# Attention's first fetches on two issuing engines, batch 1 fetched behind the first maxima's rows, and TensorE's branch moved ahead of its waits

## The reference

```python
x = x + L0_xattn(layernorm(x), ctx, ctx, mask, Wq, bq, Wk, bk, Wv, bv, Wo, bo)   # key mask
x = x + L0_ffn(layernorm(x), ternary_weight, bias, act_scale)
x = x + L1_xattn(layernorm(x), ctx, ctx, W_q, W_k, W_v, b_v, W_o, b_o)           # strictly causal, row 0 sees key 0
x = x + L1_ffn(layernorm(x), w_gate, w_up, w_down)                               # gated, fake-quantized
```

## Time and profile before

| | us |
|---|---|
| median of 3 runs | 1466.51 |
| lowest and highest | 1465.78, 1467.19 |
| the profiled execution | 1467.55 |
| its span, first to last instruction | 1465.8 |
| mean granted TensorE clock in it | 0.946 of full speed |

### The profile page before, as it was taken

How to read it: one execution, slowest core, us unless ns; L and a number is a source line. 1 busy time by engine, 2 the same in 40 slices (tenths; PEclk the granted TensorE clock), 3 DMA queues, 4 the chain that set the end, 5 groups by cost and what they waited for, 6 DMA issues and landing times. The chain is left out here.

```text
span 1465.8 us, 21139 instructions
## 1 busy us (share of the span) xinstructions
PE 1307.9 (89%) x7327; PEld 643.9 (44%) x7327; DVE 951.1 (65%) x1647; ACT 849.5 (58%) x1489; POOL 424.0 (29%) x639
## 2 busy tenths in 40 slices
PE   8999945999999999999999989999995999970498
PEld 4655521333434434344455445544543444430387
DVE  5444415888787887877666687877762343996532
ACT  3544420777676776777755655555553446869432
POOL 0000000013543444345465433333331001648300
PEclk9999975999999999999999999999996999985699
DMA  8768656132342434423424553333210001316132
GB/s 293 248 252 289 239 166 188 45 96 60 94 122 75 121 84 121 123 80 88 111 83 120 154 153 88 96 112 96 57 39 17 0 0 43 133 82 258 43 101 86
DMA packets 87916, 170.75 MB, mean 116 GB/s; under 512 B 14586, under 2 KB 49157, under 8 KB 86277
## 3 DMA queue, kind: packets, MB, share of 16 engines
q1 hardware_dynamic: 87812, 169.42, 37.1%
HBM read 108.27 MB, written 60.31 MB: 115 GB/s over the span
## 5 line engine op out<-in xcount | busy, mean ns | idle before, releaser
L1202 DVE TENSOR_REDUCE b_neg_max<-b_score 128x1 f32<-128x512 f32 (+3 forms) x864 | 540.6, 663 | 218.6 <-PE b_score L765 108.5
L987 ACT ACTIVATE b_probs<-b_exp 128x512 f32<-128x512 f32 (+1 forms) x864 | 463.1, 582 | 307.5 <-PE b_exp L790 306.6
L765 PE MATMUL b_score<-b_k_stack,b_q_stack 97*128 97x512 bf16 (+3 forms) x1024 | 356.7, 352 | 34.1 <-issue 21.0
L790 PE MATMUL b_exp<-b_q_stack,b_k_stack 100*128 100x512 bf16 (+3 forms) x1024 | 345.0, 342 | 20.7 <-DMA b_q_stack<-b_max_rows 15.1
L811 PE MATMUL b_av<-b_probs,b_values 128*17 128x512 f32 (+3 forms) x2048 | 229.9, 521 | 3.6 <-POOL b_probs L1080 3.3
L765 PEld LDWEIGHTS b_score<-b_k_stack,b_q_stack 97*128 97x128 bf16 x1024 | 100.0, 98 | 271.0 <-DVE b_neg_max L1202 140.4
L1088 POOL CAST b_max_parts<-b_neg_max 128x16 bf16<-128x16 f32 x64 | 12.7, 198 | 506.6 <-DVE b_neg_max L1202 506.3
L790 PEld LDWEIGHTS b_exp<-b_q_stack,b_k_stack 100*128 100x128 bf16 x1024 | 100.4, 99 | 97.7 <-ACT b_probs L987 23.7
L1080 POOL TENSOR_SCALAR_AFFINE_SELECT b_probs<-b_probs 128x512 f32<-128x512 f32 x96 | 61.7, 643 | 184.6 <-ACT b_probs L987 184.3
L768 PE MATMUL b_score<-diag_qk,minus_big 128*128 128x128 bf16 x512 | 113.0, 221 | 0.0
L1746 PE MATMUL f_down<-f_w_downT,f_tmp 128*128 128x256 f32 x384 | 84.7, 384 | 4.6 <-DVE f_tmp L1423 4.6
(11 more groups left out here) (211 smaller groups left out, 1760.2 us busy)
## 6 DMA issues: line engine op xcount, KB each, us to landing
b_q_stack<-s_q SPq DMA_DIRECT2D x384, 64.0 KB
s_k<-a_part_k SPq DMA_DIRECT2D x48, 256.0 KB, 5.6
b_k_stack<-s_k SPq DMA_DIRECT2D x64, 192.0 KB
s_up<-f_up SPq DMA_DIRECT2D x6, 1536.0 KB, 5.1
s_va<-a_va SPq DMA_DIRECT2D x16, 544.0 KB, 5.0
b_values<-s_va SPq DMA_DIRECT2D x16, 544.0 KB, 4.3
a_mask_q<-mask_in SPq DMA_DIRECT2D x8, 1024.0 KB, 7.6
b_k_stack<-s_k SPq DMA_DIRECT2D x64, 128.0 KB
```

The source lines that it names most:

```text
L765: mm = pe.matmul(o, q, KS[half][0:R_MAX, h, 0:w], start=True, stop=causal or not general)
L790: mm = pe.matmul(o, k, QS[half][0:NSTACK, h, q0:T], start=True, stop=not masked)
L987: nc.scalar.activation(probs[kc][:, h0:h0 + m, q0:T], exp_bank[n % RINGS][:, 0:m * w].rearrange("p (h n) -> p h n", h=m), ACT.Exp).then_in ...
L1202: nc.vector.tensor_reduce(neg_max[u][:, qt, h0:h0 + m], score_bank[n % RINGS][:, 0:m * w].rearrange("p (h n) -> p h n", h=m), AX.X, ALU.ma ...
```

## The change

It has four parts.

1. A helper `keep_busy` issues matmuls of 128x128 weights against 128x512 constants whose result nobody reads. TensorE runs 20 of them at the end of the projections, and 20 at the start of attention's first slots, behind the branch.
2. TensorE reads the flag and branches first. The wait on `preset` stands behind the branch and the 20 matmuls; the wait on the rows of ones moves into the maxima, for groups 0 and 4 alone, and `rows_set` becomes one semaphore for each half of the stacks.
3. The first fetches are divided: SyncE issues the queries of batch 0's four groups, with values and masks behind group 1, and x; ScalarE issues keys and rows of ones, those of the second half last.
4. Batch 1's stacks are fetched by SyncE in slots -1 (groups 0, 1) and 0 (groups 2, 3, values, masks), in each behind the sending of the maxima's rows.

```diff
+def keep_busy(pe, const, psum, count):
+    for _ in range(count):
+        pe.matmul(psum[:, :], const["ident_b"][:, :], const["less"][:, :], start=True, stop=True)
@@ project_phase, tensor
             less(NB - 1, "q0", 2)
+            keep_busy(pe, const, out(NB - 1, 7), 20)
@@ attention_phase
-        ROWS_SET = 16 * 4
+        ROWS_SET = 16 * 2
+        def fetch_queries(eng, n, g):
+            h0, h1 = 4 * g, 4 * g + 4
+            for row, i in ((0, 0), (1, 0), (2, 0), (3, 1), (4, 1), (5, 2)):
+                eng.dma_start(QS[n % 2][HD * row:HD * (row + 1), h0:h1, :], scratch["q"][n][i][:, h0:h1, :]).then_inc(stack_landed[n % 2][g], 16)
+        def fetch_keys(eng, n, g):
...
+        def constant_rows(eng, half):
+            d = scratch["one"]
+            for dst, n in ((QS[half][R_KEY:R_KEY + 1, :, :], 1), (KS[half][R_MAX:NSTACK, :, :], NSTACK - R_MAX)):
+                eng.dma_start(dst, bass.AP(d.tensor, d.offset, [[0, n], [0, H], [1, T]])).then_inc(rows_set[half], 16)
@@ sync, slot(t), behind the maxima's rows
+                if t in (-1, 0):
+                    for g in (0, 1) if t < 0 else (2, 3):
+                        fetch_stacks(1, g)
+                    if t == 0:
+                        fetch_values(1)
+                        fetch_masks(1)
@@ sync, ahead of the slots
-            fetch_stacks(0, 0)
-            for half in range(2):
...
-            fetch_values(1)
-            fetch_masks(1)
             for g in range(G):
+                fetch_queries(sp, 0, g)
+                if g == 1:
+                    fetch_values(0)
+                    fetch_masks(0)
@@ tensor
                     if s == 0:
                         pe.wait_ge(stack_landed[half][g], 16 * NLOADS * (n // 2 + 1))
+                    if s == 0 and t in (0, G):
+                        pe.wait_ge(rows_set[half], ROWS_SET)
...
+                if slots[0] < 0:
+                    keep_busy(pe, const, exp_bank[0], 20)
+                    pe.wait_ge(preset, PRESETS)
                 for t in slots:
                     slot(t)
-            pe.wait_ge(preset, PRESETS)
-            pe.wait_ge(rows_set, ROWS_SET)
             flag = pe.value_load(const["general"][0:1, 0:1])
@@ scalar, ahead of the slots
+            fetch_keys(act, 0, 0)
+            constant_rows(act, 0)
+            for g in range(1, G):
+                fetch_keys(act, 0, g)
+            constant_rows(act, 1)
```

More of the change, by code:

```diff
@@ L550, in attention_phase @@
         XQT = normed[:, 7, 0:TT * D // 2].bitcast(BF16).rearrange("p (c n) -> p c n", c=DC)
-        preset, rows_set = sem("preset"), sem("rows_set")
+        preset, rows_set = sem("preset"), [sem(f"rows_set{i}") for i in range(2)]
         stack_landed = [[sem(f"stack_landed{i}{g}") for g in range(G)] for i in range(2)]
@@ L650, in attention_phase @@
         FFN_LOAD = 41
+        def fetch_queries(eng, n, g):
[3 more added lines that the diff above has]
+        def fetch_keys(eng, n, g):
+            k, half = scratch["k"][n], n % 2
+            h0, h1 = 4 * g, 4 * g + 4
+            for row, m in ((0, 3), (3, 2), (5, 1)):
+                eng.dma_start(KS[half][HD * row:HD * (row + m), h0:h1, :], k[0:m].rearrange("i d h n -> (i d) h n")[:, h0:h1, :]).then_inc(stack_landed[half][g], 16)
+            d = scratch["dead"][n]
+            eng.dma_start(KS[half][R_KEY:R_KEY + 1, h0:h1, :], bass.AP(d.tensor, d.offset, [[0, 1], [0, h1 - h0], [1, T]])).then_inc(stack_landed[half][g], 16)
+        def constant_rows(eng, half):
+            d = scratch["one"]
+            for dst, n in ((QS[half][R_KEY:R_KEY + 1, :, :], 1), (KS[half][R_MAX:NSTACK, :, :], NSTACK - R_MAX)):
+                eng.dma_start(dst, bass.AP(d.tensor, d.offset, [[0, n], [0, H], [1, T]])).then_inc(rows_set[half], 16)
         block = mem.enter_context(nc.Block())
@@ L656, in fetch_stacks @@
             def fetch_stacks(n, g):
[L658 to L666, removed]
+                fetch_queries(sp, n, g)
+                fetch_keys(sp, n, g)
             def fetch_values(n):
@@ L672, in fetch_masks @@
                 sp.dma_start(DQ[b % 2][:, :, :], scratch["dq"][b]).then_inc(masks_landed[b % 2], 16)
-            def constant_row(name, n):
-                d = scratch[name]
-                return bass.AP(d.tensor, d.offset, [[0, n], [0, H], [1, T]])
             def slot(t):
@@ L726, in slot @@
                     ffn.load(sp)
-            fetch_stacks(0, 0)
-            for half in range(2):
[L730 to L735, removed]
             for g in range(G):
-                fetch_stacks(1, g)
-            fetch_values(1)
-            fetch_masks(1)
+                fetch_queries(sp, 0, g)
+                if g == 1:
+                    fetch_values(0)
+                    fetch_masks(0)
             sp.dma_start(XL[:, :, :], rows(dram["x"], 0)).then_inc(x_landed[0], 16)
```

## The result

The changed kernel takes 1446.1 us (median of 4 runs, 1445.1 to 1448.8) against 1466.9 (4 runs, 1465.8 to 1467.3): a ratio of 0.9861, 95% interval 0.9849 to 0.9873, 20.7 us less. 1447.7 was forecast. The profiled execution took 1445.1 us with a span of 1443.4, 22.4 less than before.

What follows compares the result with a forecast made beforehand. TensorE, busy 89% of 1465.8 us, had its hole at the seam between projections and attention. Gaining 19.8 us at the first exponent, less 0.5 for late rows and 0.5 for clock, gave 18.8 us: 1447.7 us, range 1443 to 1453.5.

Steps and rivals of the forecast that it cites:

- Term 1: End of projections: twenty matmuls add 4.4 us, hidden by the stores before the barrier; 0.15 us charged.
- Term 2: Start of attention: branch ahead of the waits moves the first score matmul from 219.15 to 214.4, 4.8 us gained.
- Term 3: Before the first exponent: the 15.1 us wait for the maxima's rows vanishes; start moves from 253.7 to 233.9.
- Term 4: Slots 0 to 2: later rows in time by 0.4 to 2 us; 0.5 us charged for them, 0.5 for the clock.
- late rows: Rival, slots 1 and 2: maxima's rows stand behind batch 1's fetches, 2 to 4 us each, 1453 us; chance 0.12.
- The sum: Whole kernel: 19.8 us at the first exponent less 0.5 for rows and 0.5 for clock, 18.8 us gained.
- The rule against it: First fetches: queues share 16 DMA engines, so two save only issue time, some 5 us of the rows' landing.
- an unmoved front: Rival, start of attention: first score stays near 219, gain 14.1 us, 1452.4 us; chance 0.10.
- come back as one for stacks: Rival, slots 0 and 1: the 15 us return as a wait for batch 0's stacks, no change, 1466.5; chance 0.02.
- the slower one: Rival, attention slots: low clock outlasts slot 0, up to 12.5 us per slot, 1471.7 us with two; chance 0.03.

Runs made afterwards that it cites:

- experiments 1 and 2: Changed kernel without the second twenty matmuls, 1445.8 us, ratio 0.9853; and with forty in place of the second twenty, 1452.2 us, ratio 0.9895.
- Experiment 5: Kernel before with only batch 1's fetches moved behind the maxima's rows, all DMAs still on SyncE: 1452.8 us, ratio 0.9908.
- experiments 7 and 8: Changed kernel with SyncE fetching batch 1 in the old order, 1460.2 us; changed kernel without both twenties, waits ahead of the branch, 1455.1 us.

## Why the prediction was right

- Term 1, the first twenty: ends at 202.2 (forecast 202.5); SyncE's first fetch at 202.48 is 4.97 us behind the last projection matmul, 4.91 before. The barrier was not delayed, where 0.15 was charged.
- Term 2, the branch: the place is right and two sizes are wrong, with opposite signs. From the barrier to the first helper matmul it took 6.2 us, where I took 4.4 from the kernel before, whose branch met lighter traffic. The second twenty took 5.9 us where I took 7.1: the clock rose 3 us after they began. That the two nearly cancel is luck: the first score was forecast at 214.4 and measured at 214.58. My price for a DMA issued by ScalarE, 0.5 us, was somewhat low: the first six took 3.7 us, 0.6 each. Rows of ones were there by 211.5 (forecast 211.1), and experiments 1 and 2 confirm that the matmuls and not the data set the start.
- Term 3: first exponent forecast at 233.9, measured 233.61, 19.0 us behind the first score where I took 19.5. SyncE was free at 217.7, not at 215, since its queries took 0.57 us each and not 0.44; the first rows were ready only at 228.3, so this cost nothing. Experiment 5 isolates the wait at 15.7 us against the 15.1 of the earlier trace rows.
- Term 4: no late rows in slots 1 and 2 (the wait list has no such entry), so the 0.5 charged was not needed; the second rows went out at 239.98, forecast 240.0. The low clock in slot 0 cost 1.0 us by slot 2 (first exponent to the copy at 264.15 is 30.5 us, 29.6 before), where 0.5 was charged. Over the fourteen profiled executions the clock rose 3.0 to 6.0 us behind the first exponent, and this stretch took 29.5 to 30.7 us.
- The sum, 18.8 us, against 19.2 to 19.4 at every milestone of attention. The rest of the measured 20.7, 1.3 us, lies within what the FFN's clock makes of a median of four runs; that it is nothing else is not shown.
- The rule against it: I computed that batch 0's fetches would be done by 223, at 245 GB/s, and took this for room. The DMA engines moved 217 GB/s at a share of 1.04 until 226, so there was none. It did no harm, because the first rows go out only at 228.3. In experiments 7 and 8, where something had to pass through while the engines were full, the same reading failed by 6 us.

Of the rivals, late rows and an unmoved front did not occur, and the wait did not come back as one for stacks; the slower one, a lasting low clock, did not either, since the clock rose 5.6 us into slot 0.

## What to carry to other kernels

Ask of a fetch ahead of a loop not whether it is early enough, but what stands behind it in the issuing engine's queue: moving 42 issues behind three small ones gave most of this gain by itself. A second issuing engine fills the DMA engines, and whatever needs them meanwhile, a small DMA or a branch's instructions, then waits longer; put such a thing ahead of the flood. Measure filler work meant for the clock by leaving it out: here the later twenty matmuls stood on the critical path for 3 us and nothing that followed was faster.

## What the runs showed that I had not expected

- The same branch costs 3.7 to 8.4 us, rising with the DMA share during it (0.37 to 1.05), because one 16 KB packet of instructions starts 1.1 to 5.6 us into it.
- Three row DMAs of 4 KB each landed 8.0 us behind the last one's issue with the engines full until 246, and 3.6 us at a share of 0.70.
- In an untouched phase 400 us later the mean granted clock over 60 us was 0.77, 0.80, 0.83 or 0.86 from one profiled execution to another, with 372.5, 372.1, 371.4 and 370.1 us (middle values) for the rest of the kernel: 3 us that belong to no edit.
